# Order of the loads at the start of a post-norm layer: half of x, the first weight columns, then the rest

## The reference

```python
x = _layernorm(x + attn(x, w_q, w_k, w_v, w_o))
x = _layernorm(x + ffn(x, W_exp, b_exp, up_w, up_b, down_w, W_con, b_con, down_b))

def attn(x, w_q, w_k, w_v, w_o):
    q, k, v = (einsum('BSE,EHK->BSHK', x, w) for w in (w_q, w_k, w_v))
    logits = einsum('BSHK,BMHK->BSHM', q, k) / sqrt(64)
    probs = softmax(logits + causal_mask, axis=3)
    return einsum('BSHK,EHK->BSE', einsum('BSHM,BMHK->BSHK', probs, v), w_o)

def ffn(x, W_exp, b_exp, up_w, up_b, down_w, W_con, b_con, down_b):
    h = butterfly(x @ W_exp + b_exp, up_w)          # 9 stages of 2x2 mixes
    h = butterfly(gelu(h + up_b), down_w)
    return h @ W_con + b_con + down_b
```

## Time and profile before

| what | value |
|---|---|
| median of three runs | 1101.54 us (1101.34 to 1102.37) |
| the profiled execution's own time | 1099.16 us |
| its span, first to last instruction | 1097.1 us |
| PE busy | 1057.8 us, 96% of the span |
| DVE, ACT, POOL busy | 66%, 56%, 69% |
| mean granted TensorE clock | 0.987 of full |
| first projection starts | 10.04 us |
| first max product starts | 18.25 us |
| first scores start | 42.95 us |

### The profile page before, as it was taken

The page is one execution under the profiler, slowest core; times in us unless marked ns, Lnnn a source line. Parts: engine busy times, 40 slices in busy tenths (PEclk is TensorE's granted clock), DMA queues, the critical chain, the costliest instruction groups (busy, mean ns, idle before and its releaser), DMA issues.

```text
span 1097.1 us, 17976 instructions
## 1 busy us (share of the span) xinstructions
PE 1057.8 (96%) x5816; PEld 710.8 (65%) x5816; DVE 725.7 (66%) x2029; ACT 619.2 (56%) x1246; POOL 754.8 (69%) x722
## 2 busy tenths in 40 slices
PE   4899999999999999999999999999999999998897
PEld 3566666666776666666766666666766666655566
DVE  6667767677657777676667777776667767641655
ACT  3366666666456666666456666666356666653331
POOL 6278878778457788787468777887467887776112
PEclk8799999999999999999999999999999999999999
DMA  7123222232122322222122222222122222201002
GB/s 217 39 69 78 52 70 53 73 78 60 41 68 59 79 78 52 71 51 73 39 79 54 74 59 79 78 52 69 28 59 78 79 58 69 59 21 30 1 19 59
DMA packets 59626, 68.72 MB, mean 63 GB/s; under 512 B 24807, under 2 KB 31243, under 8 KB 59534
## 3 DMA queue, kind: packets, MB, share of 16 engines
q1 hardware_dynamic: 59534, 67.58, 23.8%
HBM read 31.11 MB, written 2.36 MB: 31 GB/s over the span
## 4 chain that ended last, share of the span: by engine, by line
PE 93%; DVE 3%; POOL 1%; DMA 1%; issue 1%; ACT 1%; SPq 1%; POOLq 0%; DVEq 0%; ACTq 0%
PE O L671 24%; PE SC L646 14%; PE WORK L605 13%; PE SC L650 12%; PE WORK L621 6%; PE WORK L634 5%; PE WORK L581 3%; PE WORK L583 3%; PE WORK L733 3%; PE WORK L582 3%; PE SC L724 1%; PE WORK L591 1%; PE WORK L592 1%; PE WORK L724 1%; PE WORK L593 1%; DVE WORK L951 1%
## 5 line engine op out<-in xcount | busy, mean ns | idle before, releaser
L827 ACT ACTIVATE PR<-SC 128x512 f32<-128x512 f32 (+3 forms) x768 | 352.9, 490 | 313.9 <-PE SC L650 233.8
L484 POOL TENSOR_TENSOR SUM<-SUM,PR 128x1024 f32<-128x1024 f32 (+3 forms) x256 | 417.8, 1632 | 11.5
L646 PE MATMUL SC<-QH,KHL 128*128 128x512 f32 (+3 forms) x768 | 271.2, 359 | 3.5 <-ACT PR L827 1.9
L951 DVE CUSTOM_DVE_ANT_0 WORK<-WORK,CMASK 128x128 f32<-128x128 f32 (+3 forms) x512 | 238.7, 519 | 36.1 <-PE WORK L605 34.4
L650 PE MATMUL SC<-QL,KH 128*128 128x512 f32 (+3 forms) x768 | 261.7, 346 | 0.0
L605 PE MATMUL WORK<-KHL,QH 128*128 128x512 f32 (+3 forms) x768 | 225.2, 361 | 4.5 <-DMA KH<-KHL 2.7
L469 POOL TENSOR_SCALAR_AFFINE_SELECT PR<-PR 128x256 f32<-128x256 f32 x256 | 105.4, 412 | 160.4 <-ACT PR L827 159.9
L671 PE MATMUL O<-PR,VLO 128*64 128x512 f32 (+3 forms) x1024 | 207.0, 525 | 0.0
L646 PEld LDWEIGHTS SC<-QH,KHL 128*128 128x128 f32 x768 | 145.2, 189 | 80.3 <-ACT PR L827 46.7
L492 POOL TENSOR_TENSOR SUM<-PR 128x768 f32<-128x768 f32 x64 | 134.8, 2106 | 86.3 <-DVE OT L995 60.7
L605 PEld LDWEIGHTS WORK<-KHL,QH 128*128 128x128 f32 x768 | 132.6, 190 | 71.8 <-issue 52.8
(11 more groups left out here) (102 smaller groups left out, 1097.8 us busy)
## 6 DMA issues: line engine op xcount, KB each, us to landing
QH<-QH SPq DMA_DIRECT2D x128, 128.0 KB, 2.3
KH<-KHL SPq DMA_DIRECT2D x128, 128.0 KB, 2.3
R<-RROW SPq DMA_DIRECT2D x128, 128.0 KB, 2.8
SW<-in_L_ffn_up_weights_dram SPq DMA_DIRECT2D x9, 512.0 KB, 4.7
SW<-_L_ffn_down_weights_dram SPq DMA_DIRECT2D x9, 512.0 KB, 4.6
out_dram<-X SPq DMA_DIRECT2D x8, 256.0 KB, 2.3
QL<-NROW SPq DMA_DIRECT2D x64, 4.0 KB
RCOL<-R SPq DMA_DIRECT2D x64, 4.0 KB
```

Of the source, the lines that this page charges most:

```text
L484: nc.gpsimd.tensor_tensor(total, total, prob(unit, s), ALU.add).then_inc(add_done, 1)
L646: nc.tensor.matmul(dst, KHL[:, par, h, kt * P:(kt + 1) * P], QH[:, par, h, q0:q0 + n], start=True, stop=False)
L827: nc.scalar.activation(prob(unit, s)[:, h, :], SC[use % NSC][:, 0:n], ACT.Exp, scale=K ** -0.5).then_inc(exp_done, 1)
L951: op = nc.vector.tensor_tensor_reduce(cols, cols, CMASK[:, CH - n:], 1.0, LOWEST, ALU.add, ALU.max, cell)
```

## The change

SP issues the loads in another order. Batch 0 of x comes in two halves, each with its own semaphore (`in_x[0]` and `in_x[1]`); batches 1 to 3 now have `in_x[2]`. Between the halves stand the columns of the three weights that the first staging reads (128 of w_q, 128 of w_k, 256 of w_v) with the new semaphore `in_first`. The other columns follow behind the second half. The four loads of `w_o`, `W_con` and the bias rows move from behind L395 to directly behind batches 1 to 3 of x. The waits of PE, ACT and DVE follow the new semaphores.

```diff
-        in_x, in_w = [sem("in_x0"), sem("in_x1")], sem("in_w")
+        in_x, in_w, in_first = [sem(f"in_x{i}") for i in range(3)], sem("in_w"), sem("in_first")
@@ block.sync
-            sp.dma_start(X[:, 0:TILES, :], x_tiles[:, 0:TILES, :]).then_inc(in_x[0], 16)
-            for n, w in enumerate((w_q, w_k, w_v)):
-                sp.dma_start(WQKV[:, n, :], w.rearrange("e h k -> e (h k)")).then_inc(in_w, 16)
+            sp.dma_start(X[:, 0:TPC, :], x_tiles[:, 0:TPC, :]).then_inc(in_x[0], 16)
+            weights = [w.rearrange("e h k -> e (h k)") for w in (w_q, w_k, w_v)]
+            first = [P, P, 2 * P]
+            for n, w in enumerate(weights):
+                sp.dma_start(WQKV[:, n, 0:first[n]], w[:, 0:first[n]]).then_inc(in_first, 16)
+            sp.dma_start(X[:, TPC:TILES, :], x_tiles[:, TPC:TILES, :]).then_inc(in_x[1], 16)
+            for n, w in enumerate(weights):
+                sp.dma_start(WQKV[:, n, first[n]:], w[:, first[n]:]).then_inc(in_w, 16)
...
-            sp.dma_start(X[:, TILES:, :], x_tiles[:, TILES:, :]).then_inc(in_x[1], 16)
+            sp.dma_start(X[:, TILES:, :], x_tiles[:, TILES:, :]).then_inc(in_x[2], 16)
+            sp.dma_start(wo_nat, w_o.rearrange("e h k -> e (h k)")).then_inc(in_wo, 16)
+            sp.dma_start(wcon_nat, W_con.rearrange("(t p) d -> p t d", p=P)).then_inc(in_con, 16)
+            sp.dma_start(BC[:, :], b_con.rearrange("(a n) -> a n", a=1).broadcast_to([P, D])).then_inc(in_bc, 16)
+            sp.dma_start(down_row, down_b.rearrange("(a n) -> a n", a=1).broadcast_to([P, D])).then_inc(in_bc, 16)
...
             sp.dma_start(BROW, BLOCKS).then_inc(brow_in, 16)
-            sp.dma_start(wo_nat, w_o.rearrange("e h k -> e (h k)")).then_inc(in_wo, 16)
-            sp.dma_start(wcon_nat, W_con.rearrange("(t p) d -> p t d", p=P)).then_inc(in_con, 16)
-            sp.dma_start(BC[:, :], b_con.rearrange("(a n) -> a n", a=1).broadcast_to([P, D])).then_inc(in_bc, 16)
-            sp.dma_start(down_row, down_b.rearrange("(a n) -> a n", a=1).broadcast_to([P, D])).then_inc(in_bc, 16)
             rows(0)
@@ block.tensor, lay(n)
-                    pe.wait_ge(in_x[g >= CHUNKS], 16)
+                    pe.wait_ge(in_x[min(g, 2)], 16)
@@ block.scalar
-            act.wait_ge(in_w, 48)
+            act.wait_ge(in_first, 48)
             stage_weights(0)
             stage_v_weights(0)
...
                 if f == LAST_PROJ:
+                    if u < 0:
+                        act.wait_ge(in_w, 48)
                     stage_weights(u + 2)
@@ block.vector
-            dve.wait_ge(in_w, 48)
+            dve.wait_ge(in_first, 48)
```

## The result

The changed kernel took 1104.20 us in the median of 22 runs (1101.54 to 1107.88), the kernel before, timed beside it, 1101.74 us (22 runs, 1099.13 to 1103.40). The ratio is 1.0025 with a 95% interval of 1.0018 to 1.0031: slower by 2.75 us (2.0 to 3.4). The forecast was 1.6 us slower, 1103.1 us.

The account below looks back on a forecast made before the run. PE, busy 96% of the span, hardly stops after the first scores, so the end follows their start: 3.15 + 0.7 - 2.26 = +1.6 us, giving 1103.1 us on the median's scale (range 1099.4 to 1105.2).

Parts of the forecast that it names:

- Rival A: The forecast: copies of q and k wait behind the four moved loads, +1.6 us (-0.35 to +2.45); chance 55%.
- Rival B: Copies not held in the queue, DVE starts the maxima at 19.6 without a gap, -3.0 us; chance 13%.
- Rival D: Copies held, but PE's lower clock level ends before the scores, about -0.6 us; chance 15%.
- rival C: Copies held, loads at their slowest and PE's lower clock lasting longer, near +3.5 us; chance 17%.
- Part 1: First projection: halves of x land at 4.35 and 6.4, so it starts at 9.3, 0.7 us earlier.
- Part 2: SP queue behind: x batches 1 to 3 issued from 9.1, until about 17.0; w_o and the other moved loads until 19.5.
- the issues themselves delay nothing: SP queue: the four moved loads, issued from 10.0 to 11.95, leave SP free before ACT's first q at 12.3.
- Part 3: Copies of q and k behind the loads: first max product at 22.95 instead of 18.25, bounds 21.0 to 23.8.
- The sign that I had named: In the profile after, the copies of k take 6 us or more from issue to landing instead of 2.3.
- Part 4: DVE's maxima: start 3.15 us later, 0.7 wait at XTL, 2.26 gap at w_o gone; first scores +1.6 us.
- Part 5: What costs nothing: POOL's bias row, ready at 34.5 at the latest instead of 32.6, has 5 us of cover.

Follow-up runs that it names:

- Experiment 6: Kernel after, but only batch 1 of x ahead of the copies, batches 2 and 3 behind the small bias copy; ratio 0.9993 against the kernel before, -0.8 us.
- 4: Kernel after, but the four loads behind the copies of unit 0, x batches 2 and 3 behind L395's copy; ratio 0.9974 against the kernel before, -2.9 us.
- Experiment 8: Unchanged repeats for new profiles: kernel after with the four loads moved behind the first copies, 1102.5 us; kernel after, third profile, 1105.45 us.

## Why the prediction was right, and where it was not

**The mechanism.** Rival A, the forecast, is what happened: the copies come behind what was put ahead of them, PE's first max product is late, and DVE loses more there than it gains at w_o. Experiment 6 against 4 shows the holding in the queue by itself. Both halves of the change hold the copies: the first max product is at 22.59 with the split alone and at 21.94 with the four loads alone. In time that is +1.8 and +0.9 us (the latter not told apart from none), against 2.75 for both. Rival B (copies not held) fell with 23.02 instead of about 17.5. Rival D fell too: the granted clock rose again between 47 and 48 us, as before. The scores start later, so the lower level covers 2.8 us of them instead of 4.9 (by the clock of that window, 0.82 and 0.58; the prediction took 4.4 for the kernel before). So the longer spell of the lower clock that rival C counted on did not come either.

**Part 1.** First half of x at 4.0 (forecast 4.35), second half at 6.1 (6.4), first projection at 9.05 (9.3). Right.

**Part 2.** Batches 1 to 3 of x were issued at 9.21 (9.1), with two microseconds of few bytes behind the weights (126 and 160 GB/s from 10 to 12). Right. Wrong was the step that the issues themselves delay nothing: I gave four issues 0.5 us each, and the first took 3.86 us, so the q copies were issued at 15.64 instead of 12.3. In the first two profiles this cost nothing that can be seen, since the DMA engines were full up to 23 us anyway; the loads and the copies ended when their bytes were through.

**Part 3.** First max product at 23.02 (22.95). The sign that I had named, 6 us or more from issue to landing, did not appear (5.35 for the copy in the chain), because the copies had been held at the issue rather than in the queue. The sum came out for the reason of the bytes ahead, by a path half of which I had not seen. That it came out to the tenth is luck: the next profiles of the same kernel have 23.20 and 25.70, the last one beyond the bound of 23.8.

**Part 4.** DVE's first maximum 23.82 (23.45), wait at XTL 0.34 (0.7), no wait at WOT. Five products at the lower clock took 1.51 us, so DVE started 0.8 us behind PE and not 0.5, which makes the wait behind it shorter by about as much: the errors cancel. DVE's maxima took 15.6 us from start to end (15.25 and the 0.34). Scores 44.56 (44.5).

**Part 5.** POOL's bias row was ready at 31.96 + 1.26 = 33.2, within its bound of 34.5, and hid.

**The size.** The time rose by 2.75 us (2.0 to 3.4) and not by 1.6. That is inside the range of the whole forecast, but above the one of rival A alone (-0.35 to +2.45). The term that was mis-sized is the landing of the copies in part 3, taken as one number with bounds of 21.0 to 23.8: the three profiles have 23.0, 23.2 and 25.7. The mean of their first scores is 45.5, that of the two before 42.75, a difference of 2.8 us, which is the measured one; with three and two executions this agreement is weak evidence by itself. Experiment 8 shows that the start varies from execution to execution, together with the stall and with one or two late parts of batches 1 to 3 of x. What makes them late wasn't found.

## What to carry to other kernels

A queue that is issued in order is a schedule: a load that nobody waits for can still delay a small copy behind it, so put ahead of the first dependent copies only what is needed before them. Splitting or advancing a load is judged by what it pushes back; here the four more issues that gave 1 us at the first projection took more than that at the copies, and moving 1 MB that is needed much later gave the most. When a profiled execution lies at one end of the spread of the times, profile again before the difference is explained by one pair of traces.

## What the runs showed of the hardware

- SP's issue of a DMA stood still for 2.7 to 5.9 us when it came within 2 us behind the issue of a load of 1.6 MB in rows of 512 bytes, in all seven profiles (four kernels) with such a place. With 0.5 MB in its place, an issue directly behind it took 0.58 us (experiment 6; in the other three kernels with 0.5 MB the next issue came only 2.7 us or more behind, and none stalled), and in the kernel before, where the next issue came 4.9 and 4.6 us later (two profiles), none stalled either. The stall ended 4.8 to 7.4 us after the start of that load's issue. That the queue holds only so many rows would explain it; no run here counted them.
- Copies issued on a queue with 0.9 MB more of loads ahead took 5.0 us from the first k copy's issue to the first product that needs them, and 2.9 us without these loads; no issue stalled in either (experiments 6 and 4).
- A load's semaphore rises in 16 steps. In three profiles of seven, one or two of the 16 came 2.0 to 3.4 us behind the rest for a load of 1.6 MB; in two of these profiles the steps of the four copies behind it trail in the same number (8 and 4 of 64).
- The stretch from the last long run of products with the values to the end of the kernel took from 102.8 to 104.6 us in these profiles, whatever the kernel, with the granted clock at its lower level in different parts of it. A profile pair can differ by 2 us there.
